# A fused attention and feed-forward kernel: the second stage's orders rewritten, two small computations moved from VectorE to GpSimd

## The reference

```python
x = x + _L0_xattn_ref(_layernorm(x), ctx)    # both operands rounded to e4m3 in blocks of 128; product with ctx
x = x + _L0_ffn_ref(_layernorm(x), gate_w, up_w, down_w, gate_s, up_s, down_s)
                                             # (silu(h gate * gs) * (h up * us)) down * ds, 1408 hidden columns
x = x + _L1_xattn_ref(_layernorm(x), ctx, mask)            # softmax attention over ctx
x = x + _L1_ffn_ref(_layernorm(x), w_gate, w_up, w_down)   # Hadamard transform, 8-bit rows, ternary weights, 2048 hidden
```

## Time and profile before

| what | value |
|---|---|
| median of 3 runs | 718.99 us (717.25, 718.99, 727.83) |
| the profiled execution | 714.09 us, of which the span from first to last instruction is 712.2 |
| PE busy | 648.4 us (91%), 4055 matmuls |
| DVE busy | 567.2 us (80%) |
| ACT busy | 486.5 us (68%) |
| POOL busy | 362.8 us (51%) |
| second stage | 40.88 to 324.27 us of the span |
| mean granted TensorE clock | 0.993 of full speed |

### The profile page before, as it was taken

The page is one execution under the profiler, slowest core; times in us unless marked ns, Lnnn a source line. Parts: engine busy times, 40 slices in busy tenths (PEclk is TensorE's granted clock), DMA queues, the critical chain, the costliest instruction groups (busy, mean ns, idle before and its releaser), DMA issues.

```text
span 712.2 us, 12340 instructions
## 1 busy us (share of the span) xinstructions
PE 648.4 (91%) x4055; PEld 375.0 (53%) x4086; DVE 567.2 (80%) x1279; ACT 486.5 (68%) x991; POOL 362.8 (51%) x277
## 2 busy tenths in 40 slices
PE   1689799999999999998999999897999999999996
PEld 0366465757575766673444444453554555544543
DVE  6887897899789878448888875687888888888875
ACT  3748668766876656377787751666878888778734
POOL 2021231313131322147776740059899999899970
PEclk9999999999999999999999999999999999999999
DMA  8980323243322331717999951364576665665611
GB/s 206 242 280 20 84 84 87 77 119 82 97 85 51 86 100 53 218 49 198 254 280 300 239 122 30 59 90 75 102 114 126 129 122 103 136 130 113 111 59 44
DMA packets 173193, 88.19 MB, mean 124 GB/s; under 512 B 150610, under 2 KB 152658, under 8 KB 172116
## 3 DMA queue, kind: packets, MB, share of 16 engines
q1 hardware_dynamic: 167252, 71.94, 45.2%
q10 hardware_dynamic: 3408, 11.27, 4.9%
q0 software_dynamic: 2480, 4.33, 3.4%
HBM read 51.20 MB, written 4.19 MB: 78 GB/s over the span
## 4 chain that ended last, share of the span: by engine, by line
PE 37%; DVE 24%; ACT 19%; issue 11%; POOL 6%; DMA 1%; POOLq 0%; DVEq 0%; ACTq 0%; SPq 0%
PE ps L1769 9%; PE ps L1864 8%; PE ps L1846 7%; PE ps L1784 5%; DVE y_sm L1592 4%; ACT arena L604 3%; PE ps L1922 3%; ACT arena L666 2%; POOL arena L572 2%; POOL arena L573 2%; ACT arena L625 2%; DVE ps L1552 2%; ACT arena L679 2%; DVE arena L1286 2%; ACT arena L962 2%
## 5 line engine op out<-in xcount | busy, mean ns | idle before, releaser
L1769 PE MATMUL ps<-arena 128*128 128x256 f16 x1408 | 161.3, 273 | 12.6 <-DVE arena L1286 8.1
L1769 PEld LDWEIGHTS ps<-arena 128*128 128x128 f16 x1408 | 135.3, 98 | 40.1 <-DVE arena L1286 13.6
L500 POOL TENSOR_TENSOR arena<-arena 128x256 f16<-128x256 f32 x88 | 57.4, 671 | 189.8 <-ACT arena L686 189.5
L1922 PE MATMUL ps<-arena 128*128 128x512 bf16 x486 | 115.6, 380 | 7.5 <-ACT arena L914 4.0
L572 POOL TENSOR_TENSOR arena<-arena 128x1024 f32<-128x1024 f32 x44 | 103.8, 2359 | 31.5 <-DVE arena L1566 28.2
L573 POOL TENSOR_TENSOR arena<-arena 128x1024 f32<-128x1024 f32 x44 | 104.0, 2364 | 0.0
L1784 PE MATMUL ps<-arena 128*128 128x512 f16 x352 | 80.1, 384 | 3.9 <-POOL arena L500 3.9
L1922 PEld LDWEIGHTS ps<-arena 128*128 128x128 bf16 x512 | 47.8, 98 | 64.9 <-DVE arena L1558 7.7
L679 ACT ACTIVATE arena<-ps,gs 128x256 f32<-128x256 f32 x88 | 40.4, 465 | 42.8 <-PE ps L1769 42.7
L1286 DVE SCALAR_TENSOR_TENSOR arena<-ps,us,arena 128x256 f32<-128x256 f32 x88 | 42.1, 481 | 32.9 <-ACT arena L679 32.8
L1864 PE MATMUL ps<-arena 128*128 128x512 f16 x256 | 59.0, 385 | 3.3 <-DVE arena L1525 2.8
(11 more groups left out here) (173 smaller groups left out, 1182.3 us busy)
## 6 DMA issues: line engine op xcount, KB each, us to landing
arena<-in_ctx_t SPq DMA_DIRECT2D x5, 1024.0 KB, 6.1
arena<-in_wg_t SPq DMA_DIRECT2D x16, 256.0 KB, 3.9
arena<-in_wu_t SPq DMA_DIRECT2D x16, 256.0 KB, 4.4
arena<-in_wd_t SPq DMA_DIRECT2D x16, 256.0 KB, 5.1
arena<-in_wu_t ACTq DMA_DIRECT2D x4, 1024.0 KB, 6.1
arena<-in_wd_t ACTq DMA_DIRECT2D x4, 1024.0 KB, 6.8
out_x<-X SPq DMA_DIRECT2D x16, 256.0 KB, 2.5
X<-in_x SPq DMA_DIRECT2D x3, 1024.0 KB, 13.4
```

The lines of the kernel that those rows point to most:

```text
L500: nc.gpsimd.tensor_tensor(hl[:, c, at:at + 2 * P], b_h[n % 4], hh[:, c, at:at + 2 * P], ALU.subtract).then_inc(b_hl_r, 1)
L1769: last = M(bank(n % 2)[:, 2 * P * i:2 * P * i + 2 * P], W[:, b, c * P:c * P + P], part[:, b, at:at + 2 * P], start=(b == 0 and part is xhT ...
L1922: last = M(bank(2 * (n % 2) + i), d_qT[u][:, b, :], W[:, b, D * n:D * n + D], start=(b == 0), stop=(b == KD - 1))
```

## The change

In words: (1) each engine's second-stage order is rewritten, with group 0 and group 7 as functions of their own; (2) `b_center` and, for tiles 3 and up, `a_back_scales` are done by GpSimd with `tensor_scalar`, behind `root("b")` and behind `h_low` 0 and 3; `root("b", n1)` and its shift stand ahead of `h_low` 8, where the root stood behind `h_low` 9; (3) `context_max` is split in two halves; (4) the weight sums are issued pass by pass, by the table SUMS, 2, 2, 2, 2, 4 and 4 slices in groups 1 to 6 where it was 3, 2, 3, 2, 3 and 3, with SP's loads placed to fit; (5) `a_stats(3)` comes ahead of `first_low(1)`.

```diff
+        SUMS = (0, 0, 2, 4, 6, 8, 12, 16, 16)
@@ SP b_group
+                fresh = [k for k in range(first + 2, SUMS[g + 1] + 2) if k < NT]
+                four = SUMS[g + 1] - first == 4
                 a_turn(n0)
+                if four:
+                    w1a_load(fresh[0])
                 a_turn(n1)
+                if fresh:
+                    w1a_load(fresh[1 if four else 0])
                 b_turn(n0)
                 b_turn(n1)
+                for k in fresh[2 if four else 1:]:
+                    w1a_load(k)
@@ POOL
+            def b_center(j):
+                u = j % 2
+                wait(pool, b_xn_r, j - 1)
+                pool.wait_ge(st_rstd["b"], j + 1)
+                nc.gpsimd.tensor_scalar(shift[:, u, :], mv["b"][:, u, 0:1], -1.0, rstd["b"][:, u, :],
+                                        ALU.mult, ALU.mult).then_inc(b_shift, 1)
+            def a_back_scales(j):
+                u = j % 2
+                pool.wait_ge(a_smalls, 3 * j + 2)
+                pool.wait_ge(c_rel, 3 * (j // 4) + 1)
+                pool.wait_ge(a_add, j - 1)
+                nc.gpsimd.tensor_scalar(a_sm[:, u, 3, :], a_sm[:, u, 1, :], ctop[:, j // 4, 0:1], None, ALU.mult).then_inc(a_back_r, 1)
...
-                h_low(g, 0)
                 if more:
                     root("a", n1, 1)
+                h_low(g, 0)
+                if more and g:
+                    a_back_scales(n0)
+                for c in range(1, 4):
+                    h_low(g, c)
+                if more:
+                    a_back_scales(n1)
                 h_low(g, 4)
                 h_low(g, 5)
                 if more:
                     root("b", n0, 0)
+                    b_center(n0)
                 h_low(g, 6)
                 h_low(g, 7)
+                if more:
+                    root("b", n1, 1)
+                    b_center(n1)
                 h_low(g, 8)
                 h_low(g, 9)
-                if more:
-                    root("b", n1, 1)
                 h_low(g, 10)
@@ ACT b_group, groups 1 to 6
+                if g in (3, 5):
+                    context_done(e, 3)
                 b_silu(g, 0)
+                if even:
+                    context_magnitude(e, 1)
+                elif g == 1:
+                    context_done(1, 2)
+                else:
+                    weight_sums(g, 0, 1)
                 b_silu(g, 1)
...
                 b_high(g, 3)
+                a_scale(n1)
+                a_magnitude(n1)
                 b_silu(g, 5)
+                if even:
+                    weight_sums(g, 2, 3)
+                elif g == 1:
+                    weight_sums(g, 1, 2)
+                else:
+                    weight_sums(g, 3, 4)
+                b_high(g, 4)
+                b_silu(g, 6)
...
+                b_normal(n0)
+                b_silu(g, 10)
+                b_high(g, 8)
+                b_high(g, 9)
+                b_high(g, 10)
+                if scaling:
+                    context_scaled(following, 0)
+                b_normal(n1)
...
+                elif even:
+                    weight_sums(g, 3, 6)
+                else:
+                    weight_sums(g, 10, 12)
@@ DVE
             b_norm(1)
+            a_stats(3)
             first_low(1)
@@ DVE first_group, its end (group 0)
+                b_hidden(0, 10)
+                context_rounding(1, 1)
+                b_low(2)
+                context_rounding(1, 2)
+                b_low(3)
+                a_stats(4)
+                context_low(1, 0)
+                a_normal(4)
+                a_smalls_of(4)
+                dve.wait_ge(ds_r, 1)
+                b_down(0)
+                context_rounding(1, 3)
+                context_low(1, 1)
@@ DVE b_group, groups 1 to 6, as it is after the change
+                b_down(2 * g - 1)
+                a_rounding(n0)
+                b_hidden(g, 0)
+                if g in (3, 5):
+                    context_low(e, 3)
+                a_stats(n1)
+                b_hidden(g, 1)
...
+                    a_smalls_of(n1)
+                if even:
+                    context_rounding(e, 1)
+                if scaling:
+                    context_max(following, 1)
                 b_hidden(g, 4)
+                a_parts(n0, 0)
                 b_hidden(g, 5)
+                a_rounding(n1)
                 b_hidden(g, 6)
+                a_parts(n0, 1)
...
                 b_hidden(g, 8)
+                if scaling:
                     context_scales(following)
+                a_parts(n1, 0)
+                a_parts(n1, 1)
                 b_hidden(g, 9)
+                b_stats(n1)
                 b_hidden(g, 10)
+                b_low(n0)
+                if even:
+                    context_rounding(e, 3)
...
+            for g in range(1, PAIRS - 1):
+                if g == 6:
+                    mask_rows()
                 b_group(g)
+            last_group()
@@ PE b_group
                 gate_up_b(g, 1)
+                if g == 0:
+                    max_turn(1)
                 gate_up_b(g, 2)
...
                 gate_up_b(g, 3)
                 if g == 0:
-                    max_turn(1)
+                    max_spread(1)
                 gate_up_b(g, 4)
-                if more:
+                if more and g != 1:
                     a_product(n0)
                 gate_up_b(g, 5)
+                if g == 1:
+                    a_product(n0)
```

More of the change, by code:

```diff
@@ L1310, in b_group @@
                 if g == 1:
-                    context_rounding(1, 3)
-                if not more:
-                    weight_scales()
-                if g:
-                    b_down(2 * g - 1)
-                if g == 0:
-                    context_low(0, 0)
-                b_hidden(g, 0)
-                if more:
-                    a_rounding(n0)
-                b_hidden(g, 1)
-                if more:
-                    a_stats(n1)
-                b_hidden(g, 2)
-                if odd and following < B:
-                    context_max(following)
@@ L1342, in b_group @@
[L1342 to L1352 removed]
+                    context_low(1, 2)
+                if scaling:
+                    context_max(following, 0)
+                b_hidden(g, 2)
@@ L1356, in b_group @@
                 b_hidden(g, 6)
-                if more:
-                    a_parts(n0, 1)
-                if not more:
-                    weight_thresholds()
+                a_parts(n0, 1)
+                if scaling:
+                    context_top(following)
+                b_stats(n0)
                 b_hidden(g, 7)
-                if g == 0:
-                    context_rounding(1, 0)
-                if odd and following < B:
-                    context_top(following)
-                if more:
-                    b_stats(n0)
+                if even:
+                    context_rounding(e, 2)
@@ L1393, in b_group @@
-                if not odd and e < B and g:
-                    context_low(e, 1)
-                if more:
-                    b_center(n1)
+                b_low(n1)
                 if n0 + 2 < NT:
@@ L1399, in b_group, with last_group @@
                     a_smalls_of(n0 + 2)
-                if more:
-                    b_low(n1)
-                if g == 0:
-                    context_low(1, 1)
-                if not odd and e < B and g:
-                    context_rounding(e, 3)
-                if more:
-                    b_down(2 * g)
-                if not odd and e < B and g:
-                    context_low(e, 2)
-            context_max(1)
-            for g in range(PAIRS):
+                if even:
+                    context_low(e, 0)
+                b_down(2 * g)
+                if even:
+                    context_low(e, 1)
+                    context_low(e, 2)
+            def last_group():
+                g = PAIRS - 1
+                weight_scales()
+                b_down(2 * g - 1)
+                for c in range(7):
+                    b_hidden(g, c)
+                weight_thresholds()
+                for c in range(7, C0):
+                    b_hidden(g, c)
+            context_max(1, 0)
+            context_max(1, 1)
+            first_group()
+            for g in range(1, PAIRS - 1):
+                if g == 6:
+                    mask_rows()
                 b_group(g)
+            last_group()
             def add_readout(j, u):
```

322 lines of the change are left out of this document (164 added, 158 removed).

## The result

The changed kernel takes 712.62 us (median of 20 runs, 708.82 to 720.52) against 717.23 for the kernel before, measured beside it: a ratio of 0.9945 [0.992, 0.9971], some 4 us, which counts as no change at 2%. The forecast was 706 and a gain of 12.8 us; the time is inside the range of 699 to 714, but the gain is a third of what was foretold. The time lies inside the range only because the range reaches up to the rivals; it is no merit of the sum. The profiled execution went from 714.1 to 712.1 us and its span from 712.2 to 710.3.

The account below looks back on a forecast made before the run. TensorE, busy 648.4 of 712.2 us, was taken as the bound, so only its idle time could be won. Group gains of 15.2 us less the allowance gave 12.8, from 718.99 to 706 us; range 699 to 714.

Parts of the forecast that it names:

- a walk of 15.2: Second stage, group by group: summed gain 5.4 + 3.5 + 1.8 + 2.8 + 0.5 + 1.2 = 15.2 us.
- SP's queue: SP's new load order: waiting loads do not hold `b_turn`; slice 11 may be a microsecond late; nothing charged.
- Groups 0 and 1: 5.4 us: Gap of some 4 us moves to group 1's third chunk; gain 3.4, plus 2.0 from group 1's waits.
- Groups 2 and 4: Waits at group start and in `b_down` go; 33.2 us each, 3.5 and 2.8 less.
- They meet: `b_down` chunk 10: GpSimd's 7.8 us against TensorE's 7.75; VectorE 0.5 us behind in even groups.
- `mask_rows` "comes while VectorE waits for `b_down(11)`": Start of group 6: VectorE's mask work is covered by that wait; without the cover 0.99 us would remain.
- the 0.55 taken: Time for each shift or back scale on GpSimd, taken between bounds of 0.15 and 1.0 us.
- The allowance of 0.4 a group: Deduction for waits not looked for, in each of groups 1 to 6; 15.2 becomes 12.8 us.
- The orders don't do what they should: Rival: each gap reappears a few instructions on; 2 us gained, 717; chance 0.06.
- GpSimd becomes the wait: Rival, in `b_down`: shifts and back scales of 1.0 us, blocked by VectorE; 7.2 less gain, 713.5; chance 0.15.
- Slower: Rival: GpSimd pays for changing operation kinds, holding `h_low` and `b_down`; 15 us slower, 734; chance 0.04.
- a group above 34.5: Sign, in the second stage's group times, that the forecast is wrong: any group above 34.5 us.

Follow-up runs that it names:

- all repairs: Changed kernel with context load earlier, group 0's end lightened, `mask_rows` later, `context_done(e, 3)` behind the first silu of groups 3 and 5: 700.84 us (0.9833), again 702.72 (0.9789).
- The move alone: Kernel before, in its old orders, with only `b_center` and `a_back_scales` moved to GpSimd: 715.25 us, ratio 1.0033 to the kernel before.
- the orders alone: Changed kernel with shifts and back scales returned to VectorE, all else as in the change: 714.52 us, ratio 1.0008 to the kernel before.
- the one with the load first: Changed kernel with SP's context load of groups 0 and 2 ahead of the second load of weights: 705.92 us, ratio 0.9891 to the kernel before.

## Why the prediction was wrong, step by step

The gain of the stage in the profiles is 1.8 us against a walk of 15.2, and 12.8 after the allowance. By the prediction's steps:

- **The failed step is SP's queue, "I charge nothing".** It asked one question of the new load order, whether `b_turn` behind a waiting load is held, and it is not. But its reason, that each load waits for sums which ScalarE finishes before that point, is false for the second slice of group 2: these sums run at the group's end, until 149.56, and the load waits 4.8 us. The step did not ask who is queued behind that load, which is `ctx_load(3)`, nor who now reads its data earlier. Group 3 was forecast at 33.4 and took 39.58: 6.2 us, nearly half of the 13.4 that are missing from the walk. Both ends are shown, since moving either the load or its reader removes the gap.
- **"Groups 0 and 1: 5.4 us" was right in its mechanism and sized too well.** The gap came at the third chunk of group 1, 3.69 us for "some 4". But chunk 2 could go 43.1 us after the start of group 0 (39.56 to 82.63, where `b_hidden(1, 0)` ends) and not 41.0 (40.9 to 81.9). VectorE's work up to there was summed well, 39.1 us where the step has 39.5; it was idle for 4.0 us where the step has 1.5, 1.2 of them the foreseen wait for ScalarE. TensorE was late as well, since `b_down` of group 0 kept 1.25 us of waits that the step took away, so the gap did not grow. The clock fell as charged, but the charge of 1.0 should have been 1.8. These 2.1 and 0.8 are the difference between the 5.4 us and the 2.4 measured. That the gap could be had away by order alone, 4.1 us in these two groups, was not seen; the step took VectorE's 36 us of work as the reason.
- **Groups 2 and 4** were forecast at 33.2 each and took 33.85 and 33.86. Most of the difference is the wait in `b_down`. "They meet" was close: 0.97 us where 0.5 was expected. GpSimd needed 0.55 for the root, 0.18, 0.85 for the shift and 2.37 for three `h_low`:

```profile
139.09 0.55 POOL L478 TENSOR_TENSOR rstd_b<-ve_b,mhalf 128x1 f32<-128x1 f32 x1 [3.73 <-DVE ve_b L1160]
139.83 0.85 POOL L502 TENSOR_SCALAR shift<-mv_b,rstd_b 128x1 f32<-128x1 f32 x1 [0.18 <-POOL rstd_b L478]
140.63 2.37 POOL L517 TENSOR_TENSOR arena<-arena 128x256 f16<-128x256 f32 x3
```

  With all repairs and the shift on VectorE the wait is as long, but not because the shift is free. `h_low` 8 then starts 0.51 us behind the start of the root instead of 1.54, and the three take 3.16 us instead of 2.37, because they run beside `context_rounding` on VectorE. From the start of the root to the end of `h_low` 10 it is 3.67 us against 3.91. The root ahead of them is enough for the wait; the way out, `h_low` first, was tried and costs more. The smaller forecast held: the 0.3 to 0.5 us by which VectorE is late into the odd group is the 0.43 and 0.42 ahead of the third chunk of groups 3 and 5.
- **`mask_rows` "comes while VectorE waits for `b_down(11)`"** failed. VectorE reached it only at 254.49, 1.3 us before group 6 began, and its two rows, 3.4 us, reached past that cover and stood ahead of `b_hidden(6, 0)`:

```profile
254.49 2.27 DVE L1355 TENSOR_REDUCE vrow<-arena 1x4 f32<-1x2048 uint8 x1
256.69 1.20 DVE L1356 TENSOR_SCALAR mbias<-arena 1x2048 bf16<-1x2048 uint8 x1
...
260.46 0.48 DVE L1374 SCALAR_TENSOR_TENSOR arena<-ps,us,arena 128x256 f32<-128x256 f32 x1
```

  The prediction had named the price of a lost cover, 0.99, and left it out; it was 1.59. Group 6 took 34.59 instead of 32.8. Group 5 took 34.06 instead of 32.9 for other reasons: the 0.42 above and 0.61 ahead of `a_product(13)`, where TensorE waits for its transposed tile; why that transfer is late was not tested.
- **The moved operations were cheaper than the 0.55 taken.** Over all instances of each (minimum/median/maximum ns):

```profile
L502 POOL TENSOR_SCALAR shift<-mv_b,rstd_b x14: 264/320/847, 60.0 to 282.4; 128x1 f32<-128x1 f32 x14
```
```profile
L510 POOL TENSOR_SCALAR a_sm<-a_sm,ctop x13: 283/297/463, 52.6 to 269.2; 128x4 f32<-128x4 f32 x13
```

  ScalarE's wait for the shift fell from 23.3 us to 2.3. The move alone brings it to 10.9 and the orders alone to 4.7, and neither gained time, so it was mostly off TensorE's path, as the prediction says.
- **GpSimd and VectorE do hinder one another**, but less by the move than the prediction feared. The second operation of `context_rounding` takes 692 ns in the kernel before (691 to 693 in twelve instances; it is the partner of the 700 in the earlier trace rows). Its mean is 804 in the kernel after, with 1.19 us beside an `h_low`; it is 750 with the move alone, and 932 with the orders alone. So most of it comes from the new orders, which put the operation beside `h_low`, whichever engine has the shift. `b_low` on VectorE went from 688 to 760 ns, and to 720 with the orders alone. The rows one by one say who loses. Every stretched row overlaps an operation of the other engine, but not every row that overlaps is stretched. With the orders alone, 8 of the 12 rows take 1.04 us or more:

```profile
60.66 1.05 DVE L1192 SCALAR_TENSOR_TENSOR arena<-arena 128x512 f32<-128x512 f32 x1
```
```profile
60.44 1.80 POOL L502 TENSOR_TENSOR arena<-arena 128x256 f16<-128x256 f32 x2 [0.19 <-ACT arena L696]
```

  Here `h_low` began first: VectorE's row is 0.36 us longer and the pair of `h_low` 0.46 longer than undisturbed. In the kernel after, the shift puts `h_low` a little later, and at 133.51 VectorE's row, begun 0.06 us ahead of the pair, keeps its 0.69 while the pair takes 1.79; only 3 of the 12 rows are stretched. The rule of the Trainium skill in "SBUF — State Buffer", section "SBUF: two separate sides", that the two engines' shared port pair is locked for a whole instruction, fits these rows.
- **The allowance of 0.4 a group** was to cover waits not looked for. They were 13.4 us, most of it in two places. An allowance spread evenly does not stand for a queue that was not followed.
- **The rivals.** *The orders don't do what they should* (2 us gained, 717, chance 0.06) is nearest in the gain, 1.9 us of the span and 4 of the median, and in kind: gaps reappear a few instructions on. *GpSimd becomes the wait* has the nearest time, 713.5, by a mechanism that did not decide. *Slower* did not come: no shift took over 0.85 us.

The test that the prediction set itself, "a group above 34.5", is what showed it: groups 1, 3 and 6 (group 0, with 35.8, also missed its 33 to 35).

## What to carry to other kernels

When transfers are moved in an in-order queue, list every transfer that stands behind each new wait, and for each the earliest reader in the *new* orders of the other engines; a load that was late without harm becomes the bound when its reader is moved forward. When fill-in work is moved into the tail of a group, ask for the first instruction of the next group that stands behind it, because there is little slack there. The two late items that left TensorE idle for 3.7 and 4.0 us were paid twice, once as idle time and once as a slower clock behind it; the one of 1.6 us was paid once. If a gap sits beside an engine that is 90% busy, try spreading the work over the next chunks before taking the engine as the bound.

## What the runs showed of the hardware

After 3.69 us without a matmul the granted clock fell (0.53 from 82.7 to 86 in the kernel after), and the next 64 matmuls took 8.92 us instead of 7.15, so the idle time cost half as much again. Gaps of 0.4 to 0.5 us, even three within 7 us, were followed by matmuls at full speed (32 in 3.67 us), and so was the single one of 1.59 (48 in 5.42). In the kernel before, two waits of 1.26 and 1.20 us with 1.24 us of matmuls between them were followed by the lower clock, 0.50, so the length of one gap does not decide it alone.

GpSimd takes some 0.3 us for a `tensor_scalar` of one or four elements a row, less than for its power (0.55) and twice VectorE's 0.15, and up to 0.85 while VectorE is at work on a full tile. A context load of 1 MB took 7.7 us to land (median of three, which spread from 5.8 to 10.4) in the kernel after, 6.0 in the kernel before and 5.9 in the one with the load first.
